# Cross-attention's and the experts' weights and the context handed in with their axes swapped, split straight from the loaded tiles

## The reference

```
x = x + attn(layernorm(x), w_qkv, w_out)            # causal, 16 heads of 32
x = x + xattn(layernorm(x), ctx, ctx, wq, wk, wv, wo)
    # q = x wq^T, k = [ctx ; x wk^T], v = [ctx ; x wv^T]   (256 + 256 keys)
    # softmax(q k^T / sqrt(512)) v, then times wo^T
x = x + moe(layernorm(x), wg, W, b)                 # 8 experts, top 1
    # expert_out = x W[e]^T + b[e], times the gate of the chosen expert
```

## Time and profile before

| what | us |
|---|---|
| median of the three runs | 863.87 |
| profiled execution | 868.03 |
| its span | 866.3 |
| PE busy | 762.7 |
| DVE busy | 529.1 |
| ACT busy | 370.4 |
| POOL busy | 312.2 |

### The profile page before, as it was taken

The page is one execution under the profiler, slowest core; times in us unless marked ns, Lnnn a source line. Parts: engine busy times, 40 slices in busy tenths (PEclk is TensorE's granted clock), DMA queues, the critical chain, the costliest instruction groups (busy, mean ns, idle before and its releaser), DMA issues. The chain is left out here.

```text
span 866.3 us, 19948 instructions
## 1 busy us (share of the span) xinstructions
PE 762.7 (88%) x6424; PEld 688.1 (79%) x6425; DVE 529.1 (61%) x1557; ACT 370.4 (43%) x1145; POOL 312.2 (36%) x456
## 2 busy tenths in 40 slices
PE   4798989898989999757999999999999985739995
PEld 4787979888888888646899998989899974637884
DVE  4678685868686867546565655556464533834664
ACT  4476675757575767534423232313133220622221
POOL 3376574757565656641000101010101101124662
PEclk9999999999999999879999999999999997868998
DMA  9643343444444434306712425060502111765630
GB/s 345 147 114 94 105 101 106 93 118 93 116 93 118 93 94 115 101 1 208 286 52 72 99 23 113 8 121 20 101 30 67 59 15 49 168 163 152 199 122 24
DMA packets 49575, 90.90 MB, mean 105 GB/s; under 512 B 11390, under 2 KB 11518, under 8 KB 49408
## 3 DMA queue, kind: packets, MB, share of 16 engines
q1 hardware_dynamic: 43872, 77.80, 34.2%
q0 software_dynamic: 5664, 12.61, 4.7%
HBM read 51.95 MB, written 18.77 MB: 82 GB/s over the span
## 5 line engine op out<-in xcount | busy, mean ns | idle before, releaser
L398 ACT ACTIVATE prob<-prob,nmax 128x128 f32<-128x128 f32 (+1 forms) x256 | 114.5, 448 | 77.9 <-DVE nmax L576 77.9
L337 POOL TENSOR_TENSOR pt_part<-pt_rest,pt_part 128x384 bf16<-128x384 f32 x128 | 117.8, 921 | 10.2
L335 POOL CAST pt_part<-pt_rest 128x384 bf16<-128x384 f32 x128 | 67.4, 527 | 113.5 <-DVE pt_rest L585 112.1
L576 DVE CUSTOM_DVE_ANT_0 prob<-a_s,mask 128x128 f32<-128x128 f32 (+1 forms) x256 | 80.2, 350 | 4.1 <-PE a_s L457 3.2
L585 DVE TENSOR_TENSOR pt_rest<-a_t,pt_part 128x384 f32<-128x384 f32 x128 | 70.8, 553 | 7.2 <-ACT pt_part L408 7.0
L408 ACT CAST pt_part<-a_t 128x384 bf16<-128x384 f32 x128 | 60.6, 473 | 32.3 <-PE a_t L470 32.1
L470 PE MATMUL a_t<-ident,prob 128*128 128x128 f32 x384 | 63.5, 275 | 12.2 <-DVE pt_rest L585 11.8
L457 PE MATMUL a_s<-stack 96*128 96x256 f32 x256 | 61.8, 324 | 0.2 <-DVE nmax L576 0.2
L470 PEld LDWEIGHTS a_t<-ident,prob 128*128 128x128 f32 x384 | 45.2, 141 | 17.9 <-issue 15.3
L488 PE MATMUL a_o<-pt_part,v_part 128*32 128x256 bf16 (+1 forms) x1536 | 40.4, 258 | 14.2 <-POOL pt_part L337 13.9
L922 ACT CAST b_kt_hi<-b_bank 128x256 fp32r<-128x256 f32 (+1 forms) x48 | 20.5, 445 | 66.1 <-PE b_bank L56 65.2
(11 more groups left out here) (217 smaller groups left out, 1986.1 us busy)
## 6 DMA issues: line engine op xcount, KB each, us to landing
stack<-qk SPq DMA_DIRECT2D x192, 128.0 KB, 2.4
stage<-in_w SPq DMA_DIRECT2D x8, 1024.0 KB, 8.9
xin<-in_x SPq DMA_DIRECT2D x8, 512.0 KB, 3.6
xr<-in_x SPq DMA_DIRECT2D x8, 512.0 KB, 3.6
x<-xr SPq DMA_DIRECT2D x8, 512.0 KB, 2.8
xin<-x SPq DMA_DIRECT2D x8, 512.0 KB, 8.9
b_cin<-in_ctx SPq DMA_DIRECT2D x8, 512.0 KB, 3.5
xr<-x SPq DMA_DIRECT2D x8, 512.0 KB
```

The source lines that it names most:

```text
L335: nc.gpsimd.tensor_copy(pt_part[1][:, t % NPT, :], rest).then_inc(pt_mid_done, 1)
L337: nc.gpsimd.tensor_tensor(pt_part[2][:, t % NPT, :], rest, pt_part[1][:, t % NPT, :], ALU.subtract).then_inc(pt_done, 1)
L398: a = nc.scalar.activation(prob[:, e % NPROB, cols], prob[:, e % NPROB, cols], ACT.Exp, scale=-1.0, bias=nmax[:, e, q:q + 1], accum_out=rs ...
L576: m = nc.vector.tensor_tensor_reduce(out=prob[:, s % NPROB, cols], in0=s_ps[s % 2][:, q, 0:P * (q + 1)], in1=mask[:, P * (1 - q):], scale= ...
```

## The change

The host hands in `wq`, `wk`, `wv`, `wo` and each `W[e]` with their two axes swapped, and a second copy of the context, `ctx_t`, channels by tokens for each batch. PE's transposes of weights (16 in stage B, 32 jobs in stage C) and of the context (C0, C1) are gone, and so are those jobs' PSUM banks. ACT and DVE split from the SBUF tiles that the DMAs fill. `wv` and `wo` are split by POOL. The context's key half has a tile of its own, `cin_t`, with its own loads and semaphores. In stage C a split is one instruction for a whole expert.

```diff
-        ORDER = ("X0 X1 s0 s1 C0 C1 q0 q1 p0 p1 q2 q3 ...
+        ORDER = ("X0 X1 s0 s1 q0 q1 p0 p1 q2 q3 ...
-        PROLOGUE = ("wq0 wq1 wq2 wq3 wk0 wk1 X0 X1 wk2 wk3 q0 q1 C0 C1 q2 q3 wv0 wv1 k0 k1 wv2 wv3 k2 k3 wo0 v0 wo1 v1 "
-                    "wo2 wo3").split()
+        PROLOGUE = "X0 X1 q0 q1 q2 q3 k0 k1 k2 k3 v0 v1".split()
...
+            load_ctx_t = lambda b: sp.dma_start(cin_t[:], chunks(channels(b))).then_inc(ct_in, 16)
...
             def batch(n, more, load):
 
                 if load:
+                    sp.wait_ge(ct_split, n + 2)
+                    load_ctx_t(n + 2)
                     sp.wait_ge(xn_ready, (n + 2) * TB)
                     sp.dma_start(xin[:], batch_rows(x1, n + 2)).then_inc(x_in, 16)
                     sp.wait_ge(c_split, n + 2)
-                    sp.wait_ge(job_done, done_at("C1", n))
                     sp.dma_start(cin[:], batch_rows(ctx, n + 2)).then_inc(c_in, 16)
...
             rstd_ln2(0)
+            for i, name, done in ((2, "v", wv_split), (3, "o", wo_split)):
+                pool.wait_ge(w_in[i], 16)
+                nc.gpsimd.tensor_copy(wt_hi[name][:], raw[i][:] if i < 3 else raw[i]).then_inc(done, 1)
+                pool.wait_ge(done, 1)
+                nc.gpsimd.tensor_tensor(wt_lo[name][:], raw[i][:] if i < 3 else raw[i], wt_hi[name][:].bitcast(F32),
+                                        ALU.subtract).then_inc(done, 1)
+                if name == "v":
+                    rstd_ln2(1)
             routing.constants(nc, pool)
-            rstd_ln2(1)
...
+            def ctx_t_hi(k):
+
+                act.wait_ge(ct_in, 16 * (k + 1))
+                nc.scalar.copy(kt_hi[:, :, 0:S], cin_t[:]).then_inc(ct_hi, 1)
...
+                    if j == "s1" and order(n) is ORDER:
+                        ctx_t_hi(n + 1)
...
             for j in PROLOGUE:
                 job(j, -1)
             pe.wait_ge(wg_in, 16)
+            pe.wait_ge(wo_split, 2)
             pe.wait_ge(routing.consts, Routing.CONSTS)
...
+            def ctx_t_lo(k):
+                dve.wait_ge(ct_hi, k + 1)
+                nc.vector.tensor_tensor(kt_lo[:, :, 0:S], cin_t[:], kt_hi[:, :, 0:S].bitcast(F32),
+                                        ALU.subtract).then_inc(ct_split, 1)
...
+                    if j == "s1" and order(n) is ORDER:
+                        ctx_t_lo(n + 1)
...
-    EARLY = 8
+    EARLY = 2
...
-                sp.wait_ge(w_done, (e - STAGED + 1) * DC)
+                sp.wait_ge(w_split, e - STAGED + 1)
...
-                for c in range(DC):
-                    i = e * DC + c
-                    act.wait_ge(w_done, i + 1)
-                    nc.scalar.copy(wt_hi[:, c, e * D:(e + 1) * D], ring[i % RING][:, :]).then_inc(w_hi_done, 1)
+                act.wait_ge(w_in[e % STAGED], 16 * (e // STAGED + 1))
+                nc.scalar.copy(wt_hi[:, :, e * D:(e + 1) * D], stage[e % STAGED][:]).then_inc(w_hi_done, 1)
```

More of the change, by code:

```diff
@@ L756, in cross_attention @@
         cin, xn = sb("cin", [P, TB, D]), sb("xn", [P, TB, D])
+        cin_t = sb("cin_t", [P, DC, S])
         stats, mv = sb("stats", [P, 2, TB, 6]), sb("mv", [P, 2, TB, 2])
@@ L812, in route_after, with jobs_in, w_piece @@
             return "q3" if order(n) is ORDER else "p1"
+        def jobs_in(n):
+            return PROLOGUE if isinstance(n, int) and n < 0 else order(n)
         def bank(j, n):
[L815 to L818, removed]
+            return ring[jobs_in(n).index(j) % RING]
+        def w_piece(w, i):
+            return w[:, :, i * P:(i + 1) * P]
         def parts_of(j, n):
@@ L850, in _ @@
             sp.dma_start(xin[:], batch_rows(x1, 1)).then_inc(x_in, 16)
+            for i, done, count_of in ((0, w_split, DC), (1, w_split, 2 * DC), (2, wv_split, 2)):
+                sp.wait_ge(done, count_of)
+                sp.dma_start(stage[i][:], chunks(w[i])).then_inc(expert_in[i], 16)
+            sp.wait_ge(ct_split, 1)
+            load_ctx_t(1)
             sp.wait_ge(c_split, 1)
-            sp.wait_ge(job_done, done_at("C1", -1))
             sp.dma_start(cin[:], batch_rows(ctx, 1)).then_inc(c_in, 16)
[L855 to L859, removed]
+            sp.wait_ge(wo_split, 2)
             sp.dma_start(bias_sb[:], bass.AP(tensor=bias.tensor, offset=bias.offset, ap=[[0, P], [1, E * D]]))\
@@ L927, in ctx_hi, with w_hi_part @@
                 nc.scalar.copy(v_hi[:, 0:TB, :], cin[:]).then_inc(c_hi, 1)
+            def ctx_t_hi(k):
+                act.wait_ge(ct_in, 16 * (k + 1))
+                nc.scalar.copy(kt_hi[:, :, 0:S], cin_t[:]).then_inc(ct_hi, 1)
+            def w_hi_part(i):
+                name, piece = "qk"[i // DC], i % DC
+                if piece == 0:
+                    act.wait_ge(w_in[i // DC], 16)
+                nc.scalar.copy(w_piece(wt_hi[name], piece), w_piece(raw[i // DC], piece)).then_inc(w_hi, 1)
+            for i in range(DC):
+                w_hi_part(i)
             for j in PROLOGUE:
                 hi_part(j, -1)
-                if j == "C1":
+                if j == "X1":
+                    w_hi_part(DC)
+                if j in ("q0", "q1", "q2"):
+                    w_hi_part(DC + 1 + int(j[1]))
+                if j == "k0":
+                    ctx_t_hi(0)
+                if j == "k3":
                     ctx_hi(0)
@@ L955, in wait_bank @@
             def wait_bank(j, n):
[L957 to L961, removed]
-                else:
[L963 to L969, removed]
+                before = jobs_in(n).index(j) - RING
+                if before >= 0:
+                    last, of = jobs_in(n)[before], n
+                elif isinstance(n, int) and n < 0:
+                    return
+                else:
+                    of = n - 1
+                    there = len(jobs_in(of))
+                    last = jobs_in(of)[max(i for i in range(there) if i % RING == before + RING)]
                 if last[0] == "s":
@@ L1097, in ctx_lo, with w_lo_part @@
                                         ALU.subtract).then_inc(c_split, 1)
+            def ctx_t_lo(k):
+                dve.wait_ge(ct_hi, k + 1)
+                nc.vector.tensor_tensor(kt_lo[:, :, 0:S], cin_t[:], kt_hi[:, :, 0:S].bitcast(F32),
+                                        ALU.subtract).then_inc(ct_split, 1)
+            def w_lo_part(i):
+                name, piece = "qk"[i // DC], i % DC
+                dve.wait_ge(w_hi, i + 1)
+                nc.vector.tensor_tensor(w_piece(wt_lo[name], piece), w_piece(raw[i // DC], piece),
+                                        w_piece(wt_hi[name], piece).bitcast(F32), ALU.subtract).then_inc(w_split, 1)
+            ln2_stats(0)
+            w_lo_part(0)
+            ln2_apply(0)
+            for i in range(1, DC):
+                w_lo_part(i)
             for j in PROLOGUE:
                 lo_part(j, -1)
-                if j == "wq0":
-                    ln2_stats(0)
-                if j == "wq2":
-                    ln2_apply(0)
-                if j == "C1":
+                if j == "X1":
+                    w_lo_part(DC)
+                if j in ("q0", "q1", "q2"):
+                    w_lo_part(DC + 1 + int(j[1]))
+                if j == "q3":
+                    ln2_stats(1)
+                if j == "k0":
+                    ctx_t_lo(0)
+                if j == "k2":
+                    ln2_apply(1)
+                if j == "k3":
                     ctx_lo(0)
-                if j == "k1":
-                    ln2_stats(1)
-                if j == "k3":
-                    ln2_apply(1)
             def batch(n):
@@ L1464, in _ @@
             nc.vector.tensor_scalar(owner_i[:], owner[:], float(E - 1), None, ALU.min).then_inc(owner_done, 1)
-            for i in range(EARLY, W_JOBS):
+            for i in range(EARLY, E):
                 w_lo_part(i)
```

76 lines of the change are left out of this document (29 added, 47 removed).

## The result

The changed kernel takes 882.77 us, median of 4 runs (880.74 to 890.21), beside 864.74 (860.68 to 871.51, 4 runs) for the kernel before on the same chip: ratio 1.0207, 95% interval 1.0168 to 1.0246. That is +18.0 us by the medians. The profiled execution of after is the fastest of its four, 880.74, and that of before lies 3.3 above the new median; the two traces stand only 12.7 apart (span 879.0 against 866.3), and those 12.7 are what they can explain.

A forecast was written before the change was run, and what follows sets the result against it. PE alone was taken to bound batches 1 to 5. Against the profiled 868.03: -5.5 + 17.5 + 0.6 + 3.0 - 2.7 - 2.5 = 878.4, or +10.4; on the median 874.3 us, range 860 to 887.

The forecast's parts named there:

- C jobs: Batches 0 to 6: the context transposes C0 and C1 leave PE, 7 x 0.79 = 5.5 us less.
- The load of xin, moved: Batches 1 to 5: `xin` issued later, so PE waits 3.5 us for `onehot` at the count; 17.5 us more (10.7 to 24).
- The wait of 2.7 us: Not found in the prediction's text, which cites no skill; its wait at the count was 3.5 us (2.1 to 4.8).
- Batch 0: No count there; PE first needs DVE at y0, so the late `xin` costs 0.6 us (0 to 2).
- The clock: Batches 1 to 5: PE's wait may bring low clock behind it, 0 to 1.3 us per batch; 3 us more taken.
- The prologue: Before batch 0: POOL's chain with `wv`, `wo` and constants ends at 421.4, PE waits for it; 2.7 us less (1 to 5).
- rival D: Prologue: `xin` of batch 1 lands after 414, POOL ends after 425; 3 to 4 us above forecast; no chance of its own.
- Stage C: Earlier `place`, entries' store and last expert's split: 2.5 us less taken (1.5 to 5.2), or 0 if later expert loads hold.
- A: Batches: `xin` lands before 594 and DVE goes on, only the margin counts; 854.5 us, faster; chance 0.12.
- B: Batches: `xin` latency is 6 us and the clock falls in each batch; about 886 us; chance 0.16.
- C: Wait at its lower end, prologue and stage C at upper ends: 860 to 864 us; chance 0.20 together with the low case.

The follow-up runs named there:

- experiment 1: The changed kernel with SP loading `xin` first, ahead of the wait for the key split and of `cin_t`: 859.42 us, ratio 0.994 to the kernel before.
- experiment 2: The kernel before with one edit, SP's load of `xin` in each batch waits for the evacuation of q1: 878.04 us, ratio 1.0137.
- experiment 8: The changed kernel with both loads still behind the key split, but `xin` issued ahead of `cin_t`: 873.05 us, ratio 1.0075 to the kernel before.
- experiment 5: The changed kernel with `wv` and `wo` split by ACT and DVE in the prologue in place of POOL: 881.06 us, ratio 1.0161 to the kernel before.
- experiment 3: The changed kernel with 26 identity transposes on PE ahead of the count in batches 1 to 6: 874.57 us, ratio 1.0112 to the kernel before.
- experiment 7: The kernel before with the change in stage C alone (swapped expert weights, split straight from the loaded tiles): 864.82 us, ratio 0.9985.
- experiment 6: The changed kernel with `xin` loaded first, `choose` behind p1 in all batches, and `wv` and `wo` split by ACT and DVE: 855.28 us, ratio 0.988.
- 4: The changed kernel with `choose` and its `onehot` behind p1 in all batches, ahead of the statistics of `xin`: 858.83 us, ratio 0.9919 to the kernel before.

## Why the prediction came out as it did

**C jobs.** Predicted -5.5 in seven batches of 0.79; measured 0.75 a batch (experiment 1). Right.

**The load of xin, moved.** Right in place, mechanism and size. The issue I put at about 0.7 us behind the key split's end; it was 475.71 - 474.86 = 0.85. The latency I took as 4.7, made of 3.3 alone and 1.4 of queueing; from issue to the statistics it was 4.4. The parts were off in opposite directions: late and alone `xin` took 3.7 (experiment 2), behind the other load 4.3 (experiment 8 tells the queue's share). The wait came to 3.3 in place of 3.5, 16.7 us in place of 17.5. The wait of 2.7 us that the prediction estimated from the Trainium skill, "DMA: Bandwidth & Descriptors", section "Anatomy of one DMA — SWDGE (gpsimd) path", was too low by 0.6. That section fits transfers that GpSimd issues, while SP issues these; both had landed 5.0 us after the first issue, not 4.4.

**Batch 0.** I gave it +0.6 for a wait at y0; DVE's wait there didn't reach PE. Within the bounds (0 to 2).

**The clock: the term that was mis-sized.** Predicted 3.0 (0 to 6.5); measured 5.5 in the profiled execution of after and 11.7, above the upper end, in experiment 5, with the same waits. The upper end came from the last batch, three groups at low clock; behind a wait at the count there were up to six (654.54 to 659.73 in batch 5, 2.4 us). Experiment 3 shows the term by itself: 8.2 us by the medians, and 11 with the 2.8 that the filling adds in batch 6, each within some 5 us. What the medians leave for it is 18.0 + 5.3 (C jobs) - 16.7 (waits) + 0.3 (prologue) + 0.6 (stage C, experiment 7) = 7.5, an estimate. So it is more than twice the 3.0, and the larger part of the distance from +10.4 to +18.0. The runs of after point the same way: the granted clock over the run was 0.933, 0.928, 0.935 and 0.916 in the four executions, and the lowest one belongs to the 890.21.

**The prologue: mis-sized too.** Predicted -2.7, measured -0.3. The mechanism was named (POOL's chain ends last), and its durations were short. `xin` of batch 1 was used at 413.28, not 410.4: 1.9 of this is the later start of stage B, 1.0 the load. Behind it the copy took 2.50 and not 1.90 and the constants 2.5 and not 1.8, both while DVE was busy beside them. 1.0, 0.6 and 0.7 make the 2.4 that is missing. The result is that of rival D, whose condition (later than 414) wasn't met. Experiment 5 made the prologue 2.8 shorter.

**Stage C.** The two traces say -5.5 against my -2.5, but experiment 7 bounds the gain to -3.9 to +1.3 by medians, and the means over the traces differ by 2.8. The term isn't refuted, and isn't shown either; the reading from one pair of traces would have been the error. The reason that I gave for 0, that the load of an expert holds the chain instead, is what 7 shows, and the traces of 3 to 6 as well. What the term left out is the gather of tokens, which now waits for a split: behind the first transposed block PE waits 1.15 us for the second gather in after, 2.66 in experiment 6.

**The rest of the distance.** The traces differ by 12.7 where I summed 10.4, of which 1.9 is stage A, which nothing in the change touches; the start of the prologue's X0, the nearest mark in all of them, lies between 395.8 and 402.1 in the traces of all kernels. The medians differ by 18.0 since the profiled execution of after is its fastest, and that of before lies above its median. The forecast (slower, by a wait for `xin` paid at the count) is confirmed; it was 8 us too low, and of this the clock is the largest part that the runs show, the prologue (2.4) and stage C (1.9 by experiment 7) the next; what was forecast too high (waits and batch 0, 1.4) is set against them. How much is chance of four runs stays open.

**Rivals.** A (load in time) is excluded by the 19.5 us that DVE waits, and experiment 1 is what it would have been: 859.4, where I worked out 854.5 with too much for prologue and stage C. B comes near in price (883 against 886) but not in its reason: the waits were 3.3, not 4.8, and the clock, the prologue and stage C made up for it. That the time fell in B's part of the range is no merit of its latency. C falls with the prologue.

## What to carry to other kernels

When a load is added to a queue, look first at what is queued behind it and at how much slack that had: a transfer with 19 us of slack went to a wait of 3.3 us because it stood behind a semaphore of another stream, and exchanging two pairs of lines won 23 us. Where an engine waits, put what others need (here `onehot`) ahead of the waiting instruction; that alone won as much. And price a new wait of PE at its length plus the low clock behind it, 0 to 2.6 us each here.

## What the runs showed of the hardware that I had not expected

- With the same five waits of 3.3 us, the low clock behind them cost 5.5 us in one execution and 11.7 in another; with waits of 2.4 it cost 1.7, and with 1.9 still 3.8 (experiment 2). A wait of 3.38 cost nothing (batch 1 of after), one of 1.94 cost 1.7 (batch 1 of experiment 2).
- The idle 2.9 to 3.5 us of PE ahead of batch 0 cost nothing in the traces of after, 1 and 3, and 2.5 to 2.9 us of low clock in those of 4 and 8.
- POOL's subtraction of 4.66 us stretched a pair of DVE operations with a single large SBUF input each from 1.00 to 6.48, and one operation with two such inputs from 0.68 to 3.70.
- Loading 512 KB in rows of 1 KB took 3.5 to 3.6 us (`cin_t`), in rows of 2 KB 3.3 to 3.5 (`cin`): at this size the short rows cost nearly nothing. A second load 0.7 us behind the first landed after 4.3, and with the two exchanged `cin_t` took 4.9 (experiment 8).
- The same store of routing entries took 9.8 to 11.8 us in stage C where the chain shows it (before, after, 1, 8), and the load of 1 MB of weights up to 14.35 (experiment 2): one trace of such a stage says little.
